# A query and key transpose of two heads at once, with the copies out of PSUM in two blocks

## The reference

```python
x = x + 0.5 * ffn(layernorm(x))
x = x + attention(layernorm(x))
x = x + 0.5 * ffn(layernorm(x))          # the same weights as the first
# ffn: (silu(x @ w_gate.T) * (x @ w_up.T)) @ w_down.T, hidden width 2048
# attention: 16 heads of 32 columns
q, k, v = split(x @ w_qkv); q = q / |q|; k = k / |k|
q, k = rope(q), rope(k)                  # on the even heads only
logits = (q @ k.T) * q_gain[head]; causal mask; softmax; @ v; @ w_out
```

## Time and profile before

| what | value |
|---|---|
| median of three runs | 2886.03 us |
| the profiled execution | 2886.31 us, its span 2884.6 us |
| mean granted TensorE clock | 0.989 |
| TensorE busy | 2760.6 us (96%), 23232 matmuls |
| VectorE busy | 1773.9 us (61%) |
| ScalarE busy | 1193.5 us (41%) |
| POOL busy | 536.4 us (19%) |

### The profile page before, as it was taken

One profiled execution on the slowest core, in us unless ns is written; L12 is line 12 of the kernel. 1 busy time (PEld: TensorE's weight loads), 2 busy tenths in 40 slices (PEclk: granted clock), 3 DMA queues, 4 the chain that ended last, 5 costly groups with the idle time before them and its releaser, 6 DMA issues.

```text
span 2884.6 us, 56180 instructions
## 1 busy us (share of the span) xinstructions
PE 2760.6 (96%) x23232; PEld 2025.3 (70%) x23232; DVE 1773.9 (61%) x4156; ACT 1193.5 (41%) x2218; POOL 536.4 (19%) x820
## 2 busy tenths in 40 slices
PE   4699999999999999999999999999999999999999
PEld 4467776677677776777777777677777766777676
DVE  8655657565756565665655666565666657665643
ACT  5233444344533443344434444334443444344422
POOL 0103031303131211213012130212203031303100
PEclk8899999999999999999999999999999999999999
DMA  6000000000000000000000000000000000000000
GB/s 250 15 1 1 16 1 1 1 16 3 14 1 16 16 1 1 1 16 16 1 1 1 16 16 1 1 16 1 16 1 16 16 1 1 1 16 9 1 9 15
DMA packets 16574, 39.37 MB, mean 14 GB/s; under 512 B 1472, under 2 KB 1472, under 8 KB 15808
## 3 DMA queue, kind: packets, MB, share of 16 engines
q1 hardware_dynamic: 16320, 35.79, 3.5%
HBM read 26.35 MB, written 9.44 MB: 12 GB/s over the span
## 4 chain that ended last, share of the span: by engine, by line
PE 84%; DVE 11%; ACT 3%; issue 2%; POOL 1%; DMA 0%; SPq 0%; ACTq 0%; DVEq 0%
PE psum L1003 24%; PE psum L1005 24%; PE psum L1004 24%; PE psum L1153 2%; PE psum L1130 2%; DVE mneg L917 2%; PE psum L1165 1%; PE psum L1112 1%; PE psum L1046 1%; PE psum L1108 1%; DVE arena L865 1%; DVE arena L867 1%; DVE arena L938 1%; DVE arena L860 1%; PE psum L1131 1%
## 5 line engine op out<-in xcount | busy, mean ns | idle before, releaser
L1003 PE MATMUL psum<-arena,WG 128*128 128x256 f16 x2048 | 559.2, 273 | 1.4 <-DVE arena L860 1.4
L1005 PE MATMUL psum<-arena,WG 128*128 128x256 f16 x2048 | 559.3, 273 | 0.0
L1004 PE MATMUL psum<-arena,WG 128*128 128x256 f16 x2048 | 559.1, 273 | 0.0
L1003 PE MATMUL psum<-arena,WU 128*128 128x256 f16 x2048 | 558.7, 273 | 0.0
L1005 PE MATMUL psum<-arena,WU 128*128 128x256 f16 x2048 | 558.5, 273 | 0.0
L1004 PE MATMUL psum<-arena,WU 128*128 128x256 f16 x2048 | 558.5, 273 | 0.0
L865 DVE SCALAR_TENSOR_TENSOR arena<-arena,psum 128x256 f32<-128x256 f32 x512 | 215.1, 420 | 508.8 <-ACT arena L735 508.0
L735 ACT ACTIVATE arena<-psum,tscale 128x256 f32<-128x256 f32 x512 | 242.3, 473 | 661.1 <-PE psum L1005 660.9
L1003 PE MATMUL psum<-WD,arena 128*128 128x512 f16 x1024 | 388.6, 379 | 12.7 <-DVE arena L871 12.7
L1005 PE MATMUL psum<-WD,arena 128*128 128x512 f16 x1024 | 388.5, 379 | 0.0
L1004 PE MATMUL psum<-WD,arena 128*128 128x512 f16 x1024 | 388.4, 379 | 0.0
(11 more groups left out here) (139 smaller groups left out, 4534.8 us busy)
## 6 DMA issues: line engine op xcount, KB each, us to landing
arena<-in_L_attn_x SPq DMA_DIRECT2D x16, 512.0 KB, 3.7
out<-arena SPq DMA_DIRECT2D x16, 512.0 KB, 2.8
arena<-in_L_ffn_w_gate SPq DMA_DIRECT2D x4, 1024.0 KB, 9.3
arena<-in_L_ffn_w_up SPq DMA_DIRECT2D x4, 1024.0 KB, 9.3
WD<-in_L_ffn_w_down SPq DMA_DIRECT2D x4, 1024.0 KB, 11.6
arena<-in_L_attn_w_qkv SPq DMA_DIRECT2D x1, 3072.0 KB, 20.4
WQ<-in_L_attn_w_out SPq DMA_DIRECT2D x1, 1024.0 KB, 22.7
park<-arena SPq DMA_DIRECT2D x2, 512.0 KB, 2.8
```

The source lines that it names most:

```text
L1003: T_.matmul(o, lhs(0), rhs(0), start=first, stop=False)
L1004: T_.matmul(o, lhs(0), rhs(1), start=False, stop=False)
L1005: return T_.matmul(o, lhs(1), rhs(0), start=False, stop=last)
```

## The change

The stacked tensor is laid out anew. A query head is now 64 columns, high then low; a key head is 64 columns, low then high. Two neighbouring heads make 128 columns, and one transpose turns both: 4 transposes for the queries and 4 for the keys. In PSUM the even head of a pair then stands on partitions 0 to 63 and the odd head on 64 to 127. The third part, a second copy of the high rows, is made by the copies out of PSUM: for the even heads and then for the odd heads, one copy takes both parts (64 partitions) and one takes the high part again (32 partitions) to partitions 64 to 95. That is four copies on ScalarE for the queries and four on VectorE for the keys, each of 4 heads x 128 columns. ScalarE's three copies in `stack` become one. The heads' rows are high, low, high for queries and low, high, high for keys.

The copies are two stages: `("stack out", ..., 0)` for the even heads right behind the turn, then one beat (`fill(1)`), then `("stack out", ..., 1)` for the odd heads. Transposes of x stay out between the two. The semaphores qt_ev and kt_ev rise twice for a tile, and those who wait for them count double.

```diff
--- before.py
+++ after.py
@@ -103,7 +103,10 @@
     qn = [words("work", 2 * D + D * i, D) for i in range(2)]
     ropeU = words("work", 4 * D, D // 2)
     ropeV = words("work", 4 * D + D // 2, D // 2)
-    STK = halves("work", 5 * D, HH * ST).rearrange("p (h c) -> p h c", h=2 * HH)
+
+    stk = halves("work", 5 * D, (2 * D + 2 * HD) // 2)
+    STQ, STK = (stk[:, D * a:D * (a + 1)].rearrange("p (h c) -> p h c", h=HH) for a in range(2))
+    SThi = stk.rearrange("p (a c) -> p a c", a=2)[:, :, 0:D].rearrange("p a (h c) -> p a h c", c=2 * HD)[:, :, :, 0:HD]
 
     fH = [words("ffn", TH * i, TH) for i in range(2)]
     HP = [[halves("ffn", 2 * TH + TH * q + TH // 2 * i, TH // 2) for q in range(2)] for i in range(2)]
@@ -162,6 +165,12 @@
     def ps16(b):
         return psum[:, b * 512:(b + 1) * 512].bitcast(F16)
 
+    def stacked(key, odd):
+
+        bank = ps16(2 + key)[:, 0:D].rearrange("p (h n) -> p h n", n=P)
+        first = 2 * HD * odd
+        return bank[first + HD * key:first + HD * key + HD], bank[first:first + 2 * HD]
+
     QSEG = {3: 0, 2: 512, 0: 896, 1: 1024}
     KSEG = {0: 0, 1: 512, 3: 896, 2: 1024}
     QBANKS, KBANKS = ((3,), (2, 0), (1,)), ((0,), (1, 3), (2,))
@@ -238,7 +247,7 @@
             for stage in stages:
                 seen[stage] = at[0]
                 o.append(stage)
-                held[0] = stage[0] == "values" or held[0] and stage[0] != "y out"
+                held[0] = stage[4] == 0 if stage[0] == "stack out" else stage[0] == "values" or held[0] and stage[0] != "y out"
 
         def normalize(after, b, u, tiles):
 
@@ -328,7 +337,9 @@
                 if t:
                     put(("stack", b, hf, t - 1))
                     fill(2)
-                    bank3(("stack turn", b, hf, t - 1), ("stack out", b, hf, t - 1))
+                    bank3(("stack turn", b, hf, t - 1), ("stack out", b, hf, t - 1, 0))
+                    fill(1)
+                    put(("stack out", b, hf, t - 1, 1))
                 else:
                     fill(1)
             fill(1)
@@ -696,14 +707,13 @@
                 if t:
                     wait("kt_ps", i)
                 q3 = qn[t % 2].rearrange("p (h c) -> p h c", c=HD)
-                nc.scalar.activation(STK[:, :, 0:HD], q3, ACT.Copy)
-                nc.scalar.activation(STK[:, 0:HH, HD:2 * HD], q3[:, 0:HH, :], ACT.Copy)
-                nc.scalar.activation(STK[:, HH:2 * HH, 2 * HD:ST], q3[:, HH:2 * HH, :], ACT.Copy).then_inc(s["st_hi"], 1)
-
-            def stack_out(b, hf, t):
+                nc.scalar.activation(SThi, q3.rearrange("p (a h) c -> p a h c", a=2), ACT.Copy).then_inc(s["st_hi"], 1)
+
+            def stack_out(b, hf, t, odd):
                 wait("qt_ps", tile_no(b, hf, t) + 1)
-                nc.scalar.activation(QT[0:ST, :, t * P:(t + 1) * P], ps16(2)[0:ST, :].rearrange("p (h n) -> p h n", h=HH),
-                                     ACT.Copy).then_inc(s["qt_ev"], 1)
+                high, both = stacked(0, odd)
+                nc.scalar.activation(QT[0:2 * HD, odd::2, t * P:(t + 1) * P], both, ACT.Copy)
+                nc.scalar.activation(QT[2 * HD:ST, odd::2, t * P:(t + 1) * P], high, ACT.Copy).then_inc(s["qt_ev"], 1)
 
             def max_rows(b, hf, g):
                 wait("mt_ps", group_no(b, hf, g) + 1)
@@ -901,12 +911,14 @@
             def stack(b, hf, t):
                 wait("st_hi", tile_no(b, hf, t) + 1)
                 q3 = qn[t % 2].rearrange("p (h c) -> p h c", c=HD)
-                V_.tensor_tensor(STK[:, 0:HH, 2 * HD:ST], q3[:, 0:HH, :], STK[:, 0:HH, 0:HD], ALU.subtract)
-                V_.tensor_tensor(STK[:, HH:2 * HH, HD:2 * HD], q3[:, HH:2 * HH, :], STK[:, HH:2 * HH, 0:HD], ALU.subtract).then_inc(s["st_lo"], 1)
-
-            def stack_out(b, hf, t):
+                V_.tensor_tensor(STQ[:, :, HD:2 * HD], q3[:, 0:HH, :], STQ[:, :, 0:HD], ALU.subtract)
+                V_.tensor_tensor(STK[:, :, 0:HD], q3[:, HH:2 * HH, :], STK[:, :, HD:2 * HD], ALU.subtract).then_inc(s["st_lo"], 1)
+
+            def stack_out(b, hf, t, odd):
                 wait("kt_ps", tile_no(b, hf, t) + 1)
-                V_.tensor_copy(KT[0:ST, :, t * P:(t + 1) * P], ps16(3)[0:ST, :].rearrange("p (h n) -> p h n", h=HH)).then_inc(s["kt_ev"], 1)
+                high, both = stacked(1, odd)
+                V_.tensor_copy(KT[0:2 * HD, odd::2, t * P:(t + 1) * P], both)
+                V_.tensor_copy(KT[2 * HD:ST, odd::2, t * P:(t + 1) * P], high).then_inc(s["kt_ev"], 1)
 
             mnegv = mneg[:, :].rearrange("p (t h) -> p t h", t=TT)
             mstv = mst[:, :].rearrange("p (t h c) -> p t h c", t=TT, c=2)
@@ -1103,13 +1115,13 @@
             def stack_turn(b, hf, t):
                 i = tile_no(b, hf, t)
                 wait("st_lo", i + 1)
-                take(2, "qt_ev", i + 1)
-                for h in range(HH):
-                    ins = T_.transpose(ps16(2)[0:ST, h * P:(h + 1) * P], STK[:, h, :], ident16[:, :])
+                take(2, "qt_ev", 2 * (i + 1))
+                for m in range(HH // 2):
+                    ins = T_.transpose(ps16(2)[:, m * P:(m + 1) * P], stk[:, m * P:(m + 1) * P], ident16[:, :])
                 ins.then_inc(s["qt_ps"], 1)
-                take(3, "kt_ev", i + 1)
-                for h in range(HH):
-                    ins = T_.transpose(ps16(3)[0:ST, h * P:(h + 1) * P], STK[:, HH + h, :], ident16[:, :])
+                take(3, "kt_ev", 2 * (i + 1))
+                for m in range(HH // 2):
+                    ins = T_.transpose(ps16(3)[:, m * P:(m + 1) * P], stk[:, D + m * P:D + (m + 1) * P], ident16[:, :])
                 ins.then_inc(s["kt_ps"], 1)
 
             def bank_free(bank):
@@ -1120,8 +1132,8 @@
 
             def scores_max(b, hf, h):
                 if h == 0:
-                    wait("qt_ev", tile_no(b, hf, TT))
-                    wait("kt_ev", tile_no(b, hf, TT))
+                    wait("qt_ev", 2 * tile_no(b, hf, TT))
+                    wait("kt_ev", 2 * tile_no(b, hf, TT))
                     scored[0] = None
                 for bank, tiles in enumerate(QBANKS):
                     bank_free(bank)
```

## The result

The changed kernel takes 2904.42 us (median of four, 2902.42 to 2904.82) against 2886.18 for the kernel before: a ratio of 1.0062, 95% interval 1.0045 to 1.0080. It is slower by 18 us where 24 us faster was forecast. The profiled execution took 2904.73 us.

What follows compares the result with a forecast made beforehand. TensorE, busy 96% of the span, was taken as the bound. From 2886.3 us, less 28.7 (transposes) and 2.4 (low parts), plus 3.0 (score maxima) and 4.4 (moved pieces), came 2862.6, against the median 2862.3; range 2853 to 2876.

Steps and rivals of the forecast that it cites:

- second sign of being wrong: On TensorE: over 10 us of new waits on the copies would show the forecast wrong.
- Transposes: On TensorE: 512 transposes fall away at 0.056 us each, 28.7 us gained; bounds 6 to 42 us.
- Durations of the copies: Copies out of PSUM: 512 elements take 0.425 us on VectorE, 0.59 on ScalarE; 0.84 and 1.14 us more per turn.
- The overlap I gave to pairs: Neighbouring copies overlap: VectorE's start 0.34 us apart, a pair takes 0.77 us; ScalarE's pair takes 1.08.
- a block of copies in front of it costs 0.3 to 0.8, which fits: FFN chain from tanh to low part: copies delay it 0.3 to 0.8 us, within 0.97 us before the down.
- the rotation "cost ... nothing": POOL's rotation starts 0.84 us later; ScalarE may wait up to 0.4 us, costed at nothing; uncovered, 19 us.
- Rival B: Copies land on TensorE: a third of VectorE's 54 us becomes waiting beyond the costs, 2880 us; chance 6%.
- Pieces moved: Some 50 FFN pieces leave the heads; waits in second halves of samples 0, 1, 6, 7 cost 4.4 us.
- rival D: Heads cannot shrink: each FFN piece taken there leaves a hole, all 65 us lost, 2923 us; chance 4%.
- The moved wait of the score maxima: First score maxima wait for the second block: 0.5 us in about 6 of 16 places, 3.0 us; bounds 0 to 16.
- The turn's wait for low parts: TensorE's 3.8 us wait in 4 places loses 0.6 us each, 2.4 us gained; bound 0 to 3.8.

Runs made afterwards that it cites:

- run 11: Kernel before, its 16 transposes and order kept, each copy out of PSUM cut into the changed kernel's four shapes on both engines: 2928.99 us.
- run 1: Changed kernel with its eight copies, the two blocks directly one behind the other, no extra beat between them: 2899.45 us.
- runs 5 and 6: Changed kernel, blocks together, no extra beat; from the second sample no third-part copies on VectorE alone (5: 2891.86 us) or ScalarE alone (6: 2892.96 us).
- run 10: Kernel before with the extra beat behind each stack out in samples 2 to 5 alone: 2888.05 us.
- run 2: Kernel before, transposes and single copies untouched, with one more beat behind each stack out: 2900.64 us.
- runs 7 and 9: 7: changed kernel, blocks together, third part by DMA for tiles 0 to 2: 2874.34 us. 9: that, one beat moved behind the last tile's turn: 2877.26 us.

## Why the prediction was wrong

The forecast was 2862 us with a range of 2853 to 2876; measured are 2904. Its second sign of being wrong came: over 10 us of new waits of TensorE on the copies (11.0 by the list).

**Transposes: right.** 512 fewer at 56 ns; runs 11 and 1 differ by 29.5 us, of which some 27 are theirs.

**Durations of the copies: nearly right.** Single copies took 0.42 and 0.59 us, as estimated. The overlap I gave to pairs isn't there. VectorE's neighbours:

```profile
709.86 0.42 DVE L920 COPY arena<-psum 64x512 f16<-64x512 f16 x1
710.29 0.42 DVE L921 COPY arena<-psum 32x512 f16<-32x512 f16 x1
710.74 0.43 DVE L920 COPY arena<-psum 64x512 f16<-64x512 f16 x1
711.18 0.43 DVE L921 COPY arena<-psum 32x512 f16<-32x512 f16 x1
711.64 0.17 DVE L907 TENSOR_TENSOR rn<-rn,gain 128x8 f32<-128x8 f32 x1
```

They start 0.43 to 0.45 us apart, each after the end of the one before, where the earlier trace rows have 0.34 at the same length. By the Trainium skill's rule that I had weighed (VectorE: DVE Perf Modes, "Two Vector instructions with no wait between them") instructions that begin in another group of 32 partitions are held; the trace agrees. So a turn has 1.7 us on VectorE, not 1.53, and 2.4 on ScalarE, not 2.16.

**The step that failed: "a block of copies in front of it costs 0.3 to 0.8, which fits", and the rotation "cost ... nothing".** I set VectorE's and ScalarE's free share of a projection stretch against the added time and found room, and checked the FFN chain at one place and against one block. Where the time was lost, an engine was not full but had the wrong thing in front: L749 stood behind 2.4 us of copies though its input was ready (run 1), and the unit step, and with it POOL's rotation, stood behind 1.7 us of them (run 11). I had named up to 0.4 us of ScalarE's waiting for POOL and priced it at nothing; that wait grew from 7.8 to 30.4 us. Run 11 puts the copies at 43 us; my sum had 3.0 for them. Rival B was this mechanism; it got 6% and a third of VectorE's time alone. The 43 us are four fifths of the 54 us that I had worked out for VectorE, and runs 5 and 6 show that one engine's share is the wrong measure, since either alone holds up the chain.

**The term that was mis-sized: "Pieces moved", 4.4 us.** The extra beat costs the kernel before 14.3 us, in the samples that I named (run 10: 2 us in the others). But the mechanism is not the one that I gave, pieces that leave the heads, which is rival D's as well. I had taken the pieces for evenly divided over all beats, and the order has one burst in the first half of nearly each sample that takes them from the rest. So in the second halves of samples 0, 1, 6 and 7 not 2.6 pieces left the heads each, but 5, 0, 1 and 2, and samples 1 and 6, with 0 and 1, have 11 of the 14.3 us. What the runs show there are a last turn with one piece less in front, moved small waits, and a clock that drops after waits (up to 5.1 us over the run). In the changed kernel the beat costs 5 us net; it also lets an FFN step in between the blocks, and the FFN down's excess is 8.0 us there against 13.9 in run 1.

**The moved wait of the score maxima:** 3.0 us estimated, 8.5 measured, within its bounds. **The turn's wait for low parts** should have shrunk by 2.4 us and grew by 8.4, most of it in the last turns of the scarce halves (1.9 to 3.0 us each, where 1.1 stood). Without the beat (run 1) it is 7.2 us, with the beat and single copies (run 2) 7.9; only copies and beat together give 13.9.

The terms along one path, from the table: 16 to 8 transposes with two copies an engine -21.0 (-28.7 and +7.7, in which the first sample's four copies are), third part +34.2, beat +5.0: +18.2 us. In the other order the beat has 12.2 and the third part 27.0.

What stays open: the clock's drops come after waits and are part of what is counted above. Most of these runs have one or two of 3.4 us, run 2 has three, the changed kernel's 13.6 us are the most, and runs 7 and 9 have none; but no run took them away by themselves. Nor is it shown which small waits make up the rest of the beat's cost in samples 1 and 6.

## What to carry to other kernels

In a kernel whose engines run one hand-written list, ask of every added instruction not whether its engine has time but which ready instruction stands behind it, and who waits for that one, at each place where the list puts it. Relieving one of two engines in such a chain brings little: take the work off both, here by a DMA. A filler that is spread over beats is a budget, and one more beat anywhere thins the cover where it is scarcest.

## What was not expected of the hardware

ScalarE's copies of 512 f16 elements out of PSUM at changing partitions start 0.60 us apart at 0.59 us each, while its two PSUM reads of 512 in the earlier trace rows start 0.58 apart at 0.69: no overlap at all. An SBUF-to-SBUF DMA of 64 KB in packets of 256 bytes lands in 2.1 us (median of 96), and nothing in run 7's trace shows that it disturbs the engines: no wait of TensorE is put down to it, and VectorE's steps of 128x256 take 0.42 us as in the kernel before. After one wait of 2.8 us the granted clock was at its lower level for 3.4 us.
